# Scattering the far tiles one at a time, each after the landing of the one before

## The reference, cut to what matters

```python
logits = xf @ router_w.T
probs = jax.nn.softmax(logits, axis=-1)
topk_probs, topk_idx = jax.lax.top_k(probs, TOP_K)
topk_probs = topk_probs / jnp.sum(topk_probs, axis=-1, keepdims=True)
combine = jnp.zeros((N, E), dtype=x.dtype).at[jnp.arange(N)[:, None], topk_idx].add(topk_probs)
h = gelu_new(jnp.einsum('nc,ech->neh', xf, w_fc) + b_fc)
out = jnp.einsum('neh,ehc->nec', h, w_proj) + b_proj
y = jnp.einsum('nec,ne->nc', out, combine)
```

## Time and profile before

| what | us |
|---|---|
| median of three runs | 602.07 (599.05 to 603.33) |
| the profiled execution | 599.34 |
| its span, first to last instruction | 597.6 |
| PE busy | 367.9 (62%) |
| DVE busy | 332.5 (56%) |
| POOL busy | 193.3 (32%) |
| ACT busy | 180.8 (30%) |
| scatters of L458, 48 in all | 48.4, 1.009 each |

### The profile page before, as it was taken

The page is one execution under the profiler, slowest core; times in us unless marked ns, Lnnn a source line. Parts: engine busy times, 40 slices in busy tenths (PEclk is TensorE's granted clock), DMA queues, the critical chain, the costliest instruction groups (busy, mean ns, idle before and its releaser), DMA issues.

```text
span 597.6 us, 8658 instructions
## 1 busy us (share of the span) xinstructions
PE 367.9 (62%) x2164; PEld 259.3 (43%) x2165; DVE 332.5 (56%) x974; ACT 180.8 (30%) x376; POOL 193.3 (32%) x341
## 2 busy tenths in 40 slices
PE   1843698577971769259579999614706552049890
PEld 0631234424330333013569999613603551048890
DVE  7886797696028783000755655302577988216770
ACT  0021155204520114024234544201655054024440
POOL 8010003778995006720030000573030001714441
PEclk9975598758995558669789999955957755569996
DMA  2994000000000001110012222221145000233320
GB/s 59 275 374 172 0 0 2 1 0 2 0 0 0 0 2 40 53 40 0 10 58 67 61 61 60 76 57 44 36 149 194 1 0 10 97 89 77 85 60 2
DMA packets 36217, 34.55 MB, mean 58 GB/s; under 512 B 6259, under 2 KB 26949, under 8 KB 36192
## 3 DMA queue, kind: packets, MB, share of 16 engines
q1 hardware_dynamic: 32432, 26.83, 14.5%
q0 software_dynamic: 3712, 7.44, 4.3%
q10 hardware_dynamic: 48, 0.00, 0.0%
HBM read 19.92 MB, written 14.79 MB: 58 GB/s over the span
## 4 chain that ended last, share of the span: by engine, by line
PE 40%; issue 22%; DVE 19%; another core or an unknown queue 8%; ACT 2%; SPq 2%; DVEq 2%; DMA 1%; POOL 1%; ACTq 0%; POOLq 0%
PE ps L882 11%; PE ps L997 9%; PE ps L1008 9%; DVE mx L1484 4%; PE ps L856 4%; PE ps L823 3%; PE ps L871 3%; SPq L283 2%; PE ps L987 1%; DVE rs_a L1123 1%; DVE w_now L1600 1%; DVEq L1595 1%; DVE rs_a L1122 1%; ACT wmod L600 1%
## 5 line engine op out<-in xcount | busy, mean ns | idle before, releaser
L458 POOL DMA_INDIRECT rows<-token_rows,posu x48 | 48.4, 1009 | 159.2 <-DVE posu L1415 80.5
L997 PE MATMUL ps<-xsT,w_now 128*128 128x128 f32 x552 | 81.2, 294 | 28.9 <-issue 21.0
L1608 DVE TENSOR_TENSOR hb<-ps,b_in 128x512 f32<-128x512 f32 x69 | 47.6, 690 | 85.5 <-PE ps L997 51.7
L882 PE MATMUL ps<-wide,v_now 128*32 128x309 f32 (+2 forms) x256 | 76.0, 439 | 19.8 <-issue 14.3
L997 PEld LDWEIGHTS ps<-xsT,w_now 128*128 128x128 f32 x552 | 72.8, 206 | 34.7 <-issue 24.6
L1008 PE MATMUL ps<-w_out,hg 128*128 x552 | 77.8, 287 | 9.7 <-issue 6.6
L1008 PEld LDWEIGHTS ps<-w_out,hg 128*128 128x128 f32 x552 | 71.4, 202 | 9.5 <-issue 9.4
L675 ACT ACTIVATE hg<-hb 128x512 f32<-128x512 f32 x69 | 43.4, 631 | 46.7 <-DVE hb L1608 44.3
L1484 DVE TENSOR_REDUCE mx<-ps 128x512 f32 (+2 forms) x48 | 44.2, 950 | 11.1 <-PE ps L856 10.0
L882 PEld LDWEIGHTS ps<-wide,v_now 128*32 128x32 f32 x256 | 25.5, 115 | 57.0 <-issue 31.3
L1450 DVE TENSOR_SCALAR den<-ps 128x48 f32<-128x48 f32 (+1 forms) x3 | 0.6, 202 | 85.1 <-PE ps L907 85.1
(11 more groups left out here) (335 smaller groups left out, 585.6 us busy)
## 6 DMA issues: line engine op xcount, KB each, us to landing
rows<-zeros SPq DMA_DIRECT2D x22, 256.0 KB, 6.7
xs<-rows SPq DMA_DIRECT2D x69, 64.0 KB
back<-ys SPq DMA_DIRECT2D x46, 64.0 KB
w_in<-in_L_ffn_w_fc SPq DMA_DIRECT2D x1, 2048.0 KB, 14.1
w_in<-in_L_ffn_W SPq DMA_DIRECT2D x1, 2048.0 KB, 8.7
rest<-rows SPq DMA_DIRECT2D x23, 65.0 KB
token_rows<-in_L_attn_x SPq DMA_DIRECT2D x1, 832.0 KB, 8.1
wmod<-in_L_wmod SPq DMA_DIRECT2D x2, 384.0 KB, 4.1
```

Of the source, the lines that this page charges most:

```text
L458: pool.indirect_dma_start(ROWS[l], bass.IndirectOffsetOnAxis(ap=posu[:, k, j:j + 1], axis=0), token_rows[:, j, 0:WIDTH[l]], None).then_inc ...
L882: mm = pe.matmul(ps[q * OROW:(q + 1) * OROW, 6, 0:nw], v_now[:, q, jk, :], probs[:, q % 2, jk, 0:nw], start=(jk == 0), stop=(jk == nj - 1))
L997: mm = pe.matmul(ps[:, c % RING, n * P:(n + 1) * P], w_now[:, c % 2, n * P:(n + 1) * P], xsT[:, c % 2, :], start=True, stop=True)
L1608: v.tensor_tensor(hb[:, c % 2, :].rearrange("p (b t) -> p b t", b=NB), ps[:, c % RING, :].rearrange("p (b t) -> p b t", b=NB), b_in[:, l, ...
```

## The change

In `scatter_rows` a counter is kept of the scatters already sent, and for the far group every scatter after the first waits until `scattered_far` has reached 16 times that count, that is until all scatters before it have landed. The near group and the group of layer 1 are sent as before. The waits are POOL's.

```diff
@@ -453,8 +453,12 @@
                 if l:
                     pool.wait_ge(sem("gates_all"), 1)
                 pool.wait_ge(sem(f"cleared{l}"), 16 * clears(l))
+                sent = 0
                 for j in range(lo, hi):
                     for k in range(experts):
+                        if g == "far" and sent:
+                            pool.wait_ge(sem("scattered_" + g), 16 * sent)
+                        sent += 1
                         pool.indirect_dma_start(ROWS[l], bass.IndirectOffsetOnAxis(ap=posu[:, k, j:j + 1], axis=0),
                                                 token_rows[:, j, 0:WIDTH[l]], None).then_inc(sem("scattered_" + g), 16)
```

## The result

The changed kernel takes 602.34 us in the median of 20 runs (599.75 to 607.37), the kernel before 600.08 in as many. The ratio is 1.0039, with an interval of 1.0021 to 1.0056; one run of the kernel before, in the slow state at 703.23 us, is left out of it. So the change makes the kernel a little slower, by about 2.3 us, where I had forecast 0.5 us less. The profiled execution has a span of 599.7 us against 597.6 and the same granted clock (0.759 against 0.762). So 2.1 us have to be found, and behind them two changes of more than 20 us each that nearly cancel.

A forecast was written before the change was run, and what follows sets the result against it. Dense POOL scatters were taken to hold the attention pass 22.0 us; serial ones would turn that into PE waiting. PE going on at 293.20 instead of 293.69 gave -0.5 us: 598.8 profiled, 601.6 with a 2.73 offset; range 597.5 to 608.5.

The forecast's parts named there:

- The step: Start to start of POOL's far scatters: 2.35 us instead of 1.28; lower end 2.27, upper end 2.57.
- the row of 2.27: Profile row: 2.27 us from the last far scatter's start to SyncE's first load, taken as the step's lower end.
- The holds: Third attention pass: dense POOL sending delays news of PE's work, costing 22.0 us; expected to go at 41% sending.
- Where the gain went: Before the first far tile's turn: the 22 us become PE waiting, 266.7 to 288.94; only -0.5 us shows.
- After the idle time: PE's first turns after idling: 0.45 us in the second layer, 0.38 for two here; nothing counted.
- VectorE beside POOL: DVE's work after the pass, under the far scatters, may lengthen them: 1.9 us together, kept for the upper end.
- the price of L1148: By the Trainium skill, a two-port DVE operation shuts GpSimd out for its whole length: an estimated 0.86 us here.
- Everything behind it as before: After PE goes on at 293.20: loads, near scatters and gathers unchanged, only moved by -0.5 us.
- Holds that stay: Rival, third attention pass: holds continue through sending that lasts 59 us instead of 32; +22.4 us, 624.4; chance 10%.
- a fresh start for each wait: Rival, POOL's far scatters: each wait costs 0.88 us, not 0.27, step 2.88; +12.8 us, 614.8; chance 11%.
- waits that are met before they are read: Rival, POOL's added waits: they never bind, so nothing changes, 602.07 us; chance 2%.
- The faster case: Rival: far rows come sooner, so the holds' 22 us show; 6 us needs step 2.13; 596 or less; 5%.

The follow-up runs named there:

- pairs: Against the kernel before, only every second far scatter waits for all earlier ones to land; 582.89 us, ratio 0.9782.
- pace without waits: Against the kernel before, POOL fills an unused 128x512 buffer between far scatters, with no wait on a landing; 581.89 us, ratio 0.9771.
- waits without pace: Against the kernel before, each far scatter from the third waits for the one two places back, so two stay under way; 596.40 us, ratio 1.0014.
- half the bytes: Against the kernel before, far scatters are sent as densely but carry only half of each row (32 KB instead of 64 KB); 599.54 us, one run.
- the mean of fours: Against the kernel before, only every fourth far scatter waits for all earlier ones to land; 576.71 us, ratio 0.9640.
- fillers: Against the kernel before, POOL fills an unused buffer between far scatters, without waiting for landings: 128x512 gave 581.89 us, 128x256 gave 576.57 us.

## Why the prediction was wrong

**The step, the term that failed.** I took 2.35 us between far scatters, "near the lower end, because that row is of the same line". Measured: 2.504. Over 25 steps that is 3.84 us, and it is the whole miss up to the first turn (292.86 against 288.94: 3.84 from the step, 0.08 from the load to the turn, which took 2.01 for 1.93). The chain that ended last shows what the row of 2.27 was and was not (start, time, what the time went to):

```profile
283.59 2.22 DMA rows<-token_rows,posu
285.81 0.27 issue
286.08 0.96 POOL rows L462
...
288.59 2.24 DMA rows<-token_rows,posu
290.83 0.02 issue
290.85 1.88 DMA xs<-rows
```

A scatter lands 2.21 to 2.25 us after its start (the first after 2.39), whoever waits. SP then acts 0.02 us later, POOL only 0.27 us later. My lower end was the time of a scatter seen by SP, and I read SP's 2.27 as the landing with the waker's delay in it; for POOL that delay is another one. I had it in my own rows, the 0.27 from DVE's end of the slots to the near scatter, but added it only to the upper end. Had I put POOL's delay in place of SP's, the step would have been 2.25 + 0.27 = 2.52. The sign of the forecast hung on this term: by my own sum the change costs time from a step of 2.37 on, 0.02 above the 2.35 that I took, and two thirds of the range between my two ends, 2.27 and 2.57, lie beyond it. The pairs show the same two numbers for one scatter with another under way: POOL's next start 2.50 us behind it, SP's load 275.39 - 273.15 = 2.24.

The Trainium skill, "DMA: Bandwidth & Descriptors", section "Anatomy of one DMA — SWDGE (gpsimd) path", gives a fixed 2.0 us and the bytes at 436 GB/s, an estimate of 2.15 us for the landing. The trace puts it at 2.21 to 2.25. With the wake of 0.27 from the rows, that estimate led to a step of 2.42 and a turn at 290.69, some 2 us under the measured one and nearer to it than mine.

**The holds, right.** The step was to bring POOL from dense to 41% of its time, "just under the 43% of the stretch 536 to 590", and the holds to vanish: 40%, and they did. That it is the density of the sending is now shown by four cuts (pace without waits, waits without pace, half the bytes, the mean of fours); by what the dense sending does it is not shown. The place of the limit was unknown to me: between bars at 61% of the time and at 66%.

**Where the gain went, right.** PE was to idle to the first turn, with the holds' 22 us become waiting. It idled 27.35 us. That the near rows came 23.35 us sooner rather than 22 changes nothing, since the turn waits for the far rows.

**After the idle time, right.** I counted nothing for PE's idling. Its two turns took 0.91 instead of 0.38 us, at a granted clock of 0.50 (292.80 to 294.00), but from the turn to the near rows it is 4.14 us (297.00 - 292.86), against the 4.26 that I took over.

**VectorE beside POOL.** The 1.9 us in the upper end were not needed: the far scatters keep their bar of 0.96 from the third one on, where DVE finishes the attention too, and L1152 (269.43 to 270.29) falls almost wholly between two bars (268.60 to 269.56, and from 271.10). So the price of L1148 was not tested. The row at 511.83 in the earlier trace rows was a weak test as well: there the scatter had started before the copies. Where a copy of weights starts first, at 308.39 in the changed kernel, the near scatter at 308.48 takes 1.16 us instead of 0.96.

**Everything behind it as before: not quite.** I moved the rest unchanged. But the near scatters have a hold of their own, and about 1.2 us were regained around it, which I had not forecast and which no run explains: luck, as far as the runs show. So the account of the profiled execution is: -0.5 forecast, +3.8 from the step (297.00 against 293.20), -1.2 from the near hold: +2.1.

**The rivals.** Holds that stay, a fresh start for each wait (2.88 a step) and waits that are met before they are read have all fallen. The faster case needed a step of 2.13, for which a wait after every single landing is too slow: it came true with pairs (1.88 a scatter), fours and fillers.

**Two sums.** The upper end of the range should have been 607.1 + 1.9 = 609.0, not 608.5, and a loss of 6 us begins at a step of 2.61, not 2.63. Neither changes the reading.

## What to carry to other kernels

A wait that is added to thin out a train of transfers costs its count times the whole round trip, landing and the waiting engine's own delay, and that delay has to be read on the engine that will wait, not on another one that waited for the same event: 0.25 us between the two, over 25 steps, is 6 us. When a profile shows waits with no releaser beside a dense train of GpSimd transfers, try a thinner train before a serial one: here a wait at every fourth transfer gained 3.6%, a wait at each lost 0.4%. And look for the pace: here three lengths of filler bracketed it, for gathers as for scatters. What is freed at one place (23 us here) shows only if what it then waits for has not been slowed by as much.

## What the runs showed of the hardware that I had not expected

- Beside back-to-back indirect transfers of GpSimd (0.96 us of every 1.27) the news of TensorE's finished work comes late: the holds cost the pass 22 us in a train of 26 scatters, and ScalarE waited 25.6 us in one of 26 gathers. At a mean of 1.57 us a transfer no such wait is left, at 1.46 there are some. Halving the bytes (27 against 50 GB/s) leaves 23.0 of 25.1 us of them. At 1.46 the first hold comes only after some twenty transfers, which looks like a backlog that builds up; that was not tested by itself.
- The trace of dense sending is itself incomplete: of the 26 x 16 = 416 increments that the far scatters make, that of the changed kernel holds all 416, that of the kernel before 76. That would account for waits without a releaser. Lost records alone make no hold: with the filler of 512 the trace holds 322 of the 416, in fours 270, and neither pass is held. Whether the lost records and the late news of dense sending have one cause stays open.
- POOL starts on a landing 0.27 us after it, SP 0.02 us after it, in the chain of the changed kernel.
